# Normalisers spread over a head's partitions through memory and not by TensorE, with the routing moved into the batch it belongs to

## The reference, cut to what matters

```python
x = layernorm(x + attn(x))          # x: (8, 512, 128)
x = layernorm(x + moe(x))

def attn(x):                        # 16 heads of 64
    q, k, v = split(x @ W_qkv)
    q, k = relu(q @ W_f + b_f), relu(k @ W_f + b_f)
    kv = einsum('bhnd,bhne->bhde', k, v)
    out = einsum('bhnd,bhde->bhne', q, kv)
    normalizer = einsum('bhnd,bhd->bhn', q, k.sum(axis=2))
    out = out / (normalizer[..., None] + 1e-6)
    return out @ W_out + b_out

def moe(x):                         # 8 experts, the 2 best of each token
    topk_probs, topk_idx = top_k(softmax(x @ gate_w.T), 2)
    h = gelu(w1[topk_idx] @ x + b1[topk_idx])
    return sum((w2[topk_idx] @ h + b2[topk_idx]) * topk_probs)
```

## Time and profile before

| | |
|---|---|
| time, median of 3 runs | 466.5 us (465.53 to 467.39) |
| profiled execution, own time | 467.53 us |
| its span, first to last instruction | 465.7 us |
| PE busy | 435.6 us, 94% |
| DVE busy | 302.6 us, 65% |
| ACT busy | 272.3 us, 58% |
| DMA, slices 4 to 25 of 40 | below a tenth busy |

### The profile page before, as it was taken

One profiled execution on the slowest core, in us unless ns is written; L12 is line 12 of the kernel. 1 busy time (PEld: TensorE's weight loads), 2 busy tenths in 40 slices (PEclk: granted clock), 3 DMA queues, 4 the chain that ended last, 5 costly groups with the idle time before them and its releaser, 6 DMA issues.

```text
span 465.7 us, 8129 instructions
## 1 busy us (share of the span) xinstructions
PE 435.6 (94%) x2608; PEld 344.6 (74%) x2608; DVE 302.6 (65%) x899; ACT 272.3 (58%) x530; POOL 162.2 (35%) x164
## 2 busy tenths in 40 slices
PE   3999999999999999999999998999999999999940
PEld 2777776776776776776676675599999999999930
DVE  3383866986986976975975999665643222245784
ACT  2555656666665665665665663377555555555672
POOL 2101101112422421421421433067776555555550
PEclk9999999999999999999999999999999999999995
DMA  8920000000000000000000000788886987799343
GB/s 221 334 82 0 3 0 1 0 7 17 26 13 12 23 14 13 23 14 12 25 18 7 23 20 30 257 246 247 256 273 223 309 242 228 241 354 301 124 130 113
DMA packets 34442, 52.19 MB, mean 112 GB/s; under 512 B 4943, under 2 KB 24788, under 8 KB 34272
## 3 DMA queue, kind: packets, MB, share of 16 engines
q1 hardware_dynamic: 25136, 40.72, 28.5%
q0 software_dynamic: 4544, 8.54, 5.2%
q10 hardware_dynamic: 4720, 2.42, 1.8%
HBM read 39.82 MB, written 12.75 MB: 113 GB/s over the span
## 4 chain that ended last, share of the span: by engine, by line
PE 89%; DVE 4%; DMA 3%; issue 1%; ACT 1%; ACTq 1%; POOL 0%; POOLq 0%; SPq 0%; DVEq 0%
PE psA L640 14%; PE psO L532 12%; PE psG L649 9%; PE psA L434 6%; PE psA L436 6%; PE psA L435 6%; PE psS L649 6%; PE psA L511 6%; PE psG L523 3%; PE psG L554 3%; PE psG L434 3%; PE psG L435 3%; PE psA L579 3%; PE psG L436 3%; DMA bf_col<-bf 2%; PE psS L470 1%
## 5 line engine op out<-in xcount | busy, mean ns | idle before, releaser
L390 POOL DMA_INDIRECT expert_rows<-rows,pos x64 | 62.4, 976 | 114.2 <-DVE pos L1023 92.5
L415 POOL DMA_INDIRECT expert_results<-q_act,kT x56 | 55.2, 986 | 37.2 <-DVE q_act L1140 25.2
L668 ACT ACTIVATE kT<-psA,bf_col 128x512 f32<-128x512 f32 x64 | 43.9, 686 | 37.5 <-PE psA L436 37.2
L532 PE MATMUL psO<-qn,mixed 128*128 128x512 f32 x128 | 65.5, 598 | 0.0
L668 ACT ACTIVATE q_act<-psA,bf_col 128x512 f32<-128x512 f32 x64 | 43.9, 689 | 26.2 <-PE psA L436 26.1
L1054 DVE TENSOR_TENSOR qn<-q_act,psG 128x512 f32<-128x512 f32 x64 | 42.7, 680 | 5.3 <-PE psG L523 5.3
L819 DVE TENSOR_TENSOR k_lo<-psA,k_hi 128x512 fp32r<-128x512 f32 x64 | 43.5, 683 | 3.2 <-ACT k_hi L668 2.6
L511 PEld LDWEIGHTS psA<-cst,kT 128*128 128x128 f32 x256 | 31.1, 141 | 14.6 <-ACT kT L668 7.2
L434 PE MATMUL psA<-xT_hi,wk_hi 128*128 128x512 f32 x64 | 41.7, 652 | 0.0
L793 ACT ACTIVATE q_act<-psA,xT_raw 128x256 f32<-128x256 f32 x84 | 34.5, 470 | 10.7 <-PE psA L640 10.1
L511 PE MATMUL psA<-cst,kT 128*128 128x128 f32 x256 | 38.6, 273 | 1.5 <-DVE k_lo L819 1.5
(11 more groups left out here) (180 smaller groups left out, 903.1 us busy)
## 6 DMA issues: line engine op xcount, KB each, us to landing
xT_raw<-w SPq DMA_DIRECT2D x21, 578.0 KB, 4.6
x_raw<-w SPq DMA_DIRECT2D x18, 578.0 KB, 4.8
kT<-expert_rows SPq DMA_DIRECT2D x28, 132.0 KB, 4.0
x<-expert_results SPq DMA_DIRECT2D x4, 512.0 KB, 6.3
xT_raw<-xT SPq DMA_DIRECT2D x1, 1792.0 KB, 10.7
q_act<-wqkvT SPq DMA_DIRECT2D x3, 512.0 KB, 7.5
rn<-expert_rows SPq DMA_DIRECT2D x11, 132.0 KB
expert_rows<-zeros SPq DMA_DIRECT2D x9, 132.0 KB, 15.7
```

The costliest lines, as they stand in the source:

```text
L390: pool.indirect_dma_start(xs, bass.IndirectOffsetOnAxis(ap=pos_2[o % 2][:, j, k:k + 1], axis=0), rows_2[o % 2][:, j, k, :], None).then_inc ...
L415: pool.indirect_dma_start(ys, bass.IndirectOffsetOnAxis(ap=xrow[r][:, c, D:D + 1].bitcast(I32), axis=0), yrow[u][:, c, :], None, bounds_ch ...
L532: mm(psO[:, :], mixed[:, c, :], qn[:, c % 4, :], start=c == 0, stop=c == CH - 1).then_inc(o_pe, 1)
L668: return act.activation(out_, in_, func, **kw)
```

## The change

The reciprocals `rn` are written to a tensor in memory, `normalisers`, and eight transfers read them back into `bc`: each takes two rows of 512 numbers and repeats each row 64 times. The matrix `spread`, the splitting into `r_hi`, `r_rest` and `r_hl`, and `spread_norm` go away; `normalise` reads `bc`. The output of a chunk is made one chunk later in TensorE's order.

The routing of batch p moves into the second stage of batch b = p + 1: `pick` and `mark` on VectorE ahead of the reciprocals, `weigh` and `place` behind them, `ranks` between the two halves of `gram`, `exponents` and `fill` in ScalarE's second stage. `early_table` moves into the key stage of b = 7, one piece in each of the chunks 1 to 5. GpSimd's scatters go one batch earlier.

At the start TensorE does ten matmuls on zeros, the keys go ahead of the folding of the query weights (`fold_queries`, now inside the key stage of b = 0), and the constants and the bias are loaded in smaller pieces.

```diff
+        rs = nc.dram_tensor("normalisers", [P, S], F32, kind="Internal").ap()
-        spread = sb("spread", [P, CH, P], F32R)
-        r_hl = sb("r_hl", [P, S], F32R)
+        bc = sb("bc", [P, CH, S])
...
+            for b in range(B):
+                sp.wait_ge(n_step, N_STEPS * (b + 1))
+                sp.dma_start(rs, rn[:, 1, :]).then_inc(r_out, 16)
+                sp.wait_ge(r_out, 16 * (b + 1))
+                for c in range(CH):
+                    row = c % 4 * QUAD + 2 * c
+                    sp.dma_start(bc[:, c, :], rs[row:row + 2, None, :].broadcast_to([2, DH, S])).then_inc(bc_in[c], 16)
+
             sp.wait_ge(table, 2)
...
+            pe.wait_ge(zero_ready, 1)
+            for _ in range(10):
+                mm(psS[:, 0:P], zeros[:, 0, 0:P], zeros[:, 0, 0:P], start=True, stop=True)
             pe.wait_ge(in_fold, 48)
...
-                if prev:
-                    spread_norm(0)
                 for c in range(CH):
                     if cur and c and c + 1 < CH:
                         keys(c + 1)
-                    if prev and c + 1 < CH:
-                        spread_norm(c + 1)
                     if cur:
                         turn_keys(c)
-                    if prev and c:
-                        output(c - 1)
-                if old:
-                    ranks(o)
+                    if b == 0 and c == 2:
+                        fold_queries()
+                    if b == 0 and c == 3:
+                        gate_mean()
+                    if prev and c > 1:
+                        output(c - 2)
                 if prev:
+                    output(CH - 2)
                     output(CH - 1)
...
                     gram(0, (2, 3))
+                    if prev:
+                        ranks(p)
                     gram(1, (0, 1, 2, 3))
...
                 def normalise(c):
-                    dve.wait_ge(bc_pe, CH * p + c + 1)
+                    dve.wait_ge(bc_in[c], 16 * (p + 1))
                     if c >= 4:
                         dve.wait_ge(o_pe, CH * p + c - 3)
-                    dve.tensor_tensor(qn[:, c % 4, :], q_act[:, c, :], psG[:, c % 2, :], ALU.mult).then_inc(qn_done, 1)
+                    dve.tensor_tensor(qn[:, c % 4, :], q_act[:, c, :], bc[:, c, :], ALU.mult).then_inc(qn_done, 1)
...
+                    if b == B - 1 and 1 <= c <= 5:
+                        early_table(c - 1)
...
                 if cur and prev:
                     means(p)
                     scale_logits(p)
+                    router.pick()
+                    router.mark()
                 if cur:
                     dve.wait_ge(n_pe, b + 1)
...
-                    dve.wait_ge(r_h, 2 * b + 2)
-                    dve.scalar_tensor_tensor(r_hl[:, :], r_hi[:, :].bitcast(F32), con("take")[:, 0:1], r_rest[:, :],
-                                             ALU.mult, ALU.add).then_inc(r_l, 1)
+                    if prev:
+                        router.weigh()
+                        router.place()
                     mixed_second()
```

More of the change, by code:

```diff
@@ L75 @@
 for _name, _n in (("ident", P), ("tri", P), ("ones", P), ("mask", CH * 32), ("iota", E), ("dest", B * TILES * TOPK),
-                  ("first", E), ("block", NBLK), ("step", 16), ("turn", len(ERAS) * E), ("take", 2), ("spread", HD)):
+                  ("first", E), ("block", NBLK), ("step", 16), ("turn", len(ERAS) * E)):
     _C[_name] = (_at, _at + _n)
@@ L104, in shape_constants @@
     put("turn", turn[None])
[L105 to L108, removed]
     return c
@@ L192, in program @@
         endi = sb("endi", [1, E], I32)
+        past = [sb(f"past{i}", [1, LATE * len(ERAS) * E]) for i in range(2)]
         tab = sb("tab", [1, 3, NBLK])
@@ L443, in _, with fold_queries, gate_mean @@
                     last.then_inc(fold_pe, 1)
-            pe.wait_ge(in_c, 16)
-            pe.wait_ge(in_small, 64)
-            mm(psS[:, 0:E], con("ones"), gw[:, :], start=True, stop=True).then_inc(mean_pe, 1)
-            pe.wait_ge(in_fold_q, 16)
-            for c in range(CH):
-                last = mm(psG[:, c // 4, c % 4 * P:(c % 4 + 1) * P], wqkvT_sb[:, c, :], wfd[:, :], start=True, stop=True)
-            last.then_inc(fold_pe, 1)
+            def fold_queries():
+                pe.wait_ge(in_fold_q, 16)
+                for c in range(CH):
+                    last = mm(psG[:, c // 4, c % 4 * P:(c % 4 + 1) * P], wqkvT_sb[:, c, :], wfd[:, :], start=True, stop=True)
+                last.then_inc(fold_pe, 1)
+            def gate_mean():
+                pe.wait_ge(in_c, 16)
+                pe.wait_ge(in_small, 32)
+                mm(psS[:, 0:E], con("ones"), gw[:, :], start=True, stop=True).then_inc(mean_pe, 1)
             def fold_values():
@@ L502, in turn_keys @@
                         pe.wait_ge(m_first, b)
+                    if c == 0 and b == 0:
+                        pe.wait_ge(in_ident, 16)
                     if c == 1 and prev:
@@ L704, in attention @@
             def attention(b):
[L705 to L706 removed]
+                cur, prev = b < B, 1 <= b <= B
+                p = b - 1
                 def key(c):
@@ L736, in attention @@
                     hi(x_hi[:, :, :], x_raw[:, b * TILES:(b + 1) * TILES, :]).then_inc(x_h, 1)
+                if cur:
+                    key(0)
+                    if b:
+                        tokens_hi()
                 for c in range(CH):
@@ L1079, in attention @@
                         column_sums(c // 2)
-                    if old and c == 1:
-                        router.pick()
-                    if old and c == 2:
-                        router.mark()
-                    if old and c == 5:
-                        router.weigh()
+                    if b == B - 1 and 1 <= c <= 5:
+                        early_table(c - 1)
+                    if b == 0 and c == 6:
+                        dve.wait_ge(mean_pe, 1)
+                        dve.wait_ge(in_small, 32)
+                        dve.scalar_tensor_tensor(gwc[:, :], psS[:, 0:E], -1.0 / D, gw[:, :], ALU.mult, ALU.add).then_inc(gwc_ready, 1)
+                        dve.wait_ge(fold_hi, 3)
+                        lo(wq_lo[:, :], psG[:, :, :].rearrange("p a s -> p (a s)"), wq_hi[:, :]).then_inc(fold_lo, 1)
                 if cur:
@@ L1104, in attention @@
                                       ksum[:, :, None].broadcast_to([P, CH, QUAD]), ALU.mult).then_inc(ks_done, 1)
-                if b == B - 1:
-                    for part in range(3):
-                        early_table(part)
                 if cur and prev:
```

105 lines of the change are left out of this document (39 added, 66 removed).

## The result

| | before | changed |
|---|---|---|
| median of 4 runs | 466.72 us | 701.51 us (700.19 to 709.66) |
| span of the profiled execution | 465.7 us | 698.4 us |
| time between the reciprocals of two batches | 34.5 us | 62.8 us (mean of seven) |

The ratio is 1.507, with a 95% interval of 1.500 to 1.514. The prediction was 724 us, in a range from 655 to 795, so its direction and cause held and its size was 3% too high.

The account below looks back on a forecast made before the run. TensorE, busy 94% of the span, was taken to bound the kernel. 465.7 + 220.5 (periods) + 4.2 (scatters) + 37.3 (end) + 1.5 (cold start) - 5 (start) - 0.9 (table) = 723.3 us of span; median 724 us, range 655 to 795.

Parts of the forecast that it names:

- The mechanism: Attention part: two-row reads get only two transfer engines and pace the batch, TensorE near 60%; chance 0.85.
- The period: Time between the ends of the reciprocals of two batches: 66.0 us against 34.5, adding 220.5 us over seven.
- The read: Key stage: each 256 KB read takes 5.5 us on two engines, bounds 4.8 and 6.8, eight behind each other.
- The clock: Stage entered after TensorE idled: its lower clock costs 1.5 us a batch, up to 3 possible.
- The scatters' term: Four scatters share the two busy engines in each of six batches: 0.7 us each, 4.2 us in all.
- The prediction's sign of a cold start: Kernel's start: first key matmul took 0.77 us against 0.50 at b = 5, read as the 1.2 GHz clock.
- The routing: Second stage: `pick` and `mark` go ahead of the reciprocals, where VectorE idles; nothing or 0.2 us a batch.
- The end: From the last reciprocals to the first expert block: 50.3 us against 13.0, +37.3, with 1.5 for a cold start.
- The start: Kernel's start: keys begin at about 9 to 10 us, not 16.09; 5 us won, range 2 to 7.
- The table: Early table in the last batch's key stage: free while that stage waits for transfers, -0.9 us.
- Rival 1: Reads spread over sixteen engines, so the change about cancels out: 469 us (458 to 478); chance 0.10.
- Rival 2: Sixteen engines, write and read together at most 4.1 us: 2 us a batch gained, 455 us; chance 0.05.

Follow-up runs that it names:

- wide: Changed kernel with each two-row read cut into two reads of one row; 501.9 us, ratio 1.030 to the kernel before.
- four: Changed kernel with every row written twice, so a read takes four rows and repeats each 32 times; 558.7 us, one run.
- queues: Changed kernel with chunks 1, 3, 5 and 7 read by GpSimd's queue instead of SP's; 594.3 us, one run.
- ready: wide_tab without the write: its sixteen one-row reads take rows of `xT` already in memory, so values are not the true ones; 479.8 us, ratio 0.992.
- start: Kernel before with the new start alone, and two small buffers moved to memory of their own; 482.1 us, ratio 0.994.
- wide_tab: wide with the early table moved back out of the last batch's key stage; 497.8 us, ratio 1.023 to the kernel before.
- te_tab: te with the early table moved back out of the last batch's key stage; 479.7 us, ratio 0.988 to the kernel before.
- te: Changed kernel with TensorE's spreading and the output's old place put back; new start, moved routing and early table stay; 482.8 us, ratio 0.996.

## Why the prediction was right, and where it was off

**The mechanism held in every step.** The reads run on two engines (q1 at 12.9% of sixteen), VectorE's longest wait is `qn` for a transfer, 64 times, and TensorE fell to 70% of the span where I had said near 60% (it counts busy time that the lower clock stretched, below). The engines' number was the one thing that no row of before showed; `wide`, `four` and `queues` show it now. The rule that it hung on, that of the Trainium skill, "DMA: Bandwidth & Descriptors", section "Why a DMA increments its semaphore by 16 and not by 1", agrees with them for a first dimension of two, four and 64.

**The period: 66.0 predicted, 62.8 measured; with the scatters' 0.7 of its own term it is 66.7 against 62.46 for the batch shown above.** By pieces:

| piece | predicted | measured |
|---|---|---|
| N to the first multiplication | 10.3 | 9.93 |
| first to eighth (7 x 5.5, and 0.7 for scatters) | 39.2 | 36.52 |
| eighth to the end of the last output | 1.46 | 1.88 |
| from there to the next N (14.2, and 1.5 for the clock) | 15.7 | 14.13 |

- The read, **"so I take 5.5 us"**, is the term that was most mis-sized: 5.12 us, which is 131 KB / 5.12 = 25.6 KB a us for one engine. All three rows that I divided came from loads in which all sixteen were busy; none gave the rate of an engine whose neighbours idle. "On two engines I go no lower than 4.8" held. It makes 0.38 x 8 = 3.0 us a batch and 21 us in seven, of a miss of 723.3 - 698.4 = 24.9 us. The clock's 1.5 makes 10.5 more, and what came out longer than the sum (the last output by 0.4 a batch, the start, the table) gives some back.
- The scatters' term was right where it can be read: the first pair of landings is 5.8 us apart, 0.7 more than the others, in each of the six batches b = 2 to 7; behind the first N, where no scatter runs, it is 5.06.
- The clock, **"I take 1.5, as TensorE isn't wholly idle before"**, was wrong: the key stage was granted 0.75, between the two levels, but the second stage 1.00. TensorE's timeline where the one turns into the other:

```profile
273.64 3.38 PE L531 MATMUL psO<-qn,mixed 128*128 128x512 f32 x4
277.61 1.13 PE L531 MATMUL psO<-qn,mixed 128*128 128x512 f32 x2 [0.59 <-DVE qn L1054]
278.17 0.80 PE L432 MATMUL psA<-xT_hi,wq_hi 128*128 128x512 f32 x1
278.80 0.39 PE L433 MATMUL psA<-xT_lo,wq_hi 128*128 128x512 f32 x1
```

  The last output ends at 278.74, and from there to N it is 14.13 us, against 14.2 before, so nothing was lost in this stage. The first query matmul takes 0.8 us in the kernel before too, where the clock is full:

```profile
167.93 0.79 PE L434 MATMUL psA<-xT_hi,wq_hi 128*128 128x512 f32 x1
```

  What ran at 1.2 GHz were outputs inside the waiting stage (granted clock 0.54 from 273.6 to 277.0 us, 3.38 us for four, where four take 1.88 at the end of the kernel before), and there the next landing hides it. The prediction's sign of a cold start was a pace alone: the granted clock of that stretch is 1.00.
- The routing, **"Cost nothing or 0.2 a batch"**, held in most batches: T comes at N + 2.25 and not N + 2.02. In b = 2 it did not. In every kernel with the moved routing the reciprocals come 1.2 us late there (15.9 to 16.0 us from the first query matmul to N, and not 14.7), of which the next start wins back 0.7. `hot_sum`, now ahead of them, takes 1.2 us and not 0.19 while GpSimd makes `xT_lo`; in `ready`:

```profile
108.11 1.28 POOL L382 TENSOR_TENSOR xT_lo<-xT_raw,xT_hi 128x512 fp32r<-128x512 f32 x1 [4.28 <-ACT xT_hi L667]
```

```profile
108.23 1.21 DVE L995 TENSOR_TENSOR hot_sum<-hot 128x32 bf16<-128x32 f32 x1
```

  Both end together. That the one holds up the other is not shown by a run of its own.

**The end: +37.3 + 1.5 predicted, +37.7 + 0.5 measured.** The right sum hides two errors. The reads alone would have been faster than I said, but in this stage they come 5.1 to 6.4 us apart:

```profile
516.87 0.69 DVE L1054 TENSOR_TENSOR qn<-q_act,bc 128x512 f32<-128x512 f32 x1 [4.94 <-DMA bc<-normalisers]
...
522.46 0.69 DVE L1054 TENSOR_TENSOR qn<-q_act,bc 128x512 f32<-128x512 f32 x1 [4.90 <-DMA bc<-normalisers]
...
528.84 0.69 DVE L1054 TENSOR_TENSOR qn<-q_act,bc 128x512 f32<-128x512 f32 x1 [5.69 <-DMA bc<-normalisers]
```

The window of this stage has a transfer load of 0.37 and not 0.15, so other transfers (the first loads for the experts, the scatters) share the two engines. SP issued the first of those loads at 515.14 us, and the last three distances (5.6, 5.6 and 6.4 us) come behind it; still, that the loads are the cause is argued, and no run isolates it. "I add nothing" for them was right: TensorE waited for no row of theirs here.

**The start: -5 predicted, -3.85 measured**, within the 2 to 7; `start` finds -2.7 for it alone. The keys begin at 10.16 us, as said. They begin 5.9 us earlier than before, and the key stage of b = 0, which now holds `fold_queries`, takes 2.1 us longer (17.6 us from the first key matmul to the first query matmul, and 15.6 before). `fold_queries` itself takes 1.95 us and not 3.76; the new start's matmuls on zeros come before it, but no run leaves them out, and the granted clock is 1.00 in both kernels, so that they are the cause is not shown.

**The table: -0.9 predicted**, being free in a key stage that waits. The last period, which holds it, is 62.5 us, against 63.0 and 62.5 for the two before. Free it was; and it costs 4.5 us where the cover is gone. The 0.9 itself can't be seen in the periods: the last one of the kernel before is 34.5 us like the others.

**Rival 1, sixteen engines: 469 us, half a per cent over before; `wide` measured 1.030.** Its first landing was right, N + 5.6 against 5.5 measured, and so was the table. Its batch was not: it had +0.4 a batch over before, and wide_tab shows 36.7 - 34.5 = 2.2. And it had +0.2 at the end where there are 4.4: 2.0 of them are the wait for the experts' first rows behind the sixteen reads, shown above, which the sum had put at nothing. For the other 2.4 I can only argue: the last stage has no keys to fill TensorE while the write is under way, and its outputs then run at a granted clock of 0.74. **Rival 2, the faster side**, said that with a first landing by T + 2.1 a batch would gain 2 us. `ready` has its first multiplication at T + 1.9, by the instants of the kernel before, and gains 0.1 us over before in the mean (34.4 against 34.5), and 0.5 in four of its seven periods (34.0 to 34.1). That was the real error about the change: **"If nothing waited, the key stage would fall from 18.2 to 16.3 us"**. First query matmul of b = 4, first key matmul and first query matmul of b = 5 in `ready`, the window over that key stage, and the same three instants in te_tab:

```profile
166.80 0.79 PE L431 MATMUL psA<-xT_hi,wq_hi 128*128 128x512 f32 x1
...
183.77 0.50 PE L431 MATMUL psA<-xT_hi,wk_hi 128*128 128x512 f32 x1
...
200.87 0.79 PE L431 MATMUL psA<-xT_hi,wq_hi 128*128 128x512 f32 x1
```

```profile
183.50:201.00 17.50, 16.64 (x81) 10.59 (x75) 15.42 (x21) 10.08 (x18) 5.42 (x5) 1.00 0.49 131
```

```profile
148.30 0.50 PE L431 MATMUL psA<-xT_hi,wk_hi 128*128 128x512 f32 x1
...
165.78 0.79 PE L431 MATMUL psA<-xT_hi,wq_hi 128*128 128x512 f32 x1
...
182.76 0.50 PE L431 MATMUL psA<-xT_hi,wk_hi 128*128 128x512 f32 x1
```

From first key matmul to first query matmul it is 17.1 us in `ready`, 17.5 in te_tab, and 167.93 - 150.14 = 17.8 in the kernel before. So 0.3 us come from the moved routing, which te_tab has as well, and only 0.4 of the 1.9 us of spreading arrive. TensorE now has gaps (16.64 of 17.50 us busy), where before it had none. Its transposes (L520) wait over the whole of `ready` for `k_lo`, and their weight loads for ScalarE's copy of the keys (us, times, longest):

```profile
PEld psA L520 <- ACT kT L667: 18.5, 31, 1.6
PE psA L520 <- DVE k_lo L822: 5.5, 6, 1.3
```

In the second stage, from first query matmul to next key matmul, the moved routing costs 0.2 us: 17.0 in `ready` and te_tab, 184.70 - 167.93 = 16.8 before. The late reciprocals of b = 2 (a period of 35.6 us) and two longer periods at the ends take the rest.

## What to carry to other kernels

The pace of these reads on SP's queue was their bytes over the engines that the first dimension let them have: look for a short leading dimension, above all in a read that repeats few rows, and let the repeated dimension lead, or cut the read so that it does. A load line of one or two tenths under long waits for transfers is the sign. And before work is moved off the busiest engine, try the kernel with the replacement free of charge, as `ready` does: here it would have shown 0.1 us a batch over the kernel before and 0.3 over te_tab, which no path through memory was worth.

## What the runs showed of the hardware that was not expected

- One engine with idle neighbours moved 25.6 KB a us in pieces of 2 KB, two or four of them alike (131 KB in 5.12 us, 66 KB in 2.56); with sixteen busy it was 22 to 24 KB a us.
- A queue whose few engines are full holds up the one that issues. The 64 issues of the reads by SP lasted 0.5, 5.0 and 8.3 us (least, median, most), as this answer on `bc` shows, and sixteen reads on sixteen engines occupied SP's queue for 10.3 us, 0.64 each. What stood behind them in SP's order came later as well: the experts' first rows at N + 13.3 and not N + 3.3.

```profile
L320 SPq DMA_DIRECT2D bc<-normalisers x64: 498/4982/8328, 43.0 to 506.1; - x64
```

- The same read gets other engines when GpSimd's queue issues it: four under way used the time of 5.4 engines, beside SP's two, at 0.8 us of GpSimd's time for each.
- A small VectorE operation of 0.19 us took 1.2 us in a batch where it met an operation of GpSimd (`hot_sum` and `xT_lo`, b = 2 of every kernel with the moved routing, and b = 5 of te and te_tab).
